# Sorting the second list of edges later, and idle products ahead of the first one, in a graph layer followed by a mixture of experts

## The chip, the cores and the metric

The kernel runs on 1 core of one Trainium2 chip. The metric is the device time of one launch in microseconds (us). Before the change it is 717.89 us, the median of three runs.

## The reference: what is computed

```python
x = x + gnn(layernorm(x), src, dst, edge_type)      # x: 625 x 512 float32; 10625 edges, 8 types
x = x + moe(layernorm(x))                           # 16 experts, top 2, 512 -> 1024 -> 512

def gnn(input, heads, tails, rel):
    h_self = input @ W_self.T + b_self
    H_all = einsum('rod,nd->rno', W_rel, input) + b_rel[:, None, :]     # 16 relations: 8 types x 2 ways
    agg = segment_sum(H_all[rel, tails], heads, 625) + segment_sum(H_all[rel + 8, heads], tails, 625)
    return relu(h_self + agg)

def moe(x):                                         # per expert e, combine = softmax over the top two
    out += combine[:, e] * ((silu(x @ gate[e]) * (x @ up[e])) @ down[e])
```

## The kernel before

A float32 matrix is split into a high part and a remainder, and three matmuls replace one float32 matmul. Two programs follow each other.

**The round** (0 to 388 us of the profile). The 625 nodes are five tiles of 125. There are 80 *products*, one for each of the 16 relations and 5 tiles: 12 matmuls of 512 columns into `p_h` (`product`, L837 to L858). ScalarE copies the result out (`take`, L689), writes the bias of the next but one product into the same bank (`bias_in`, L695), and rounds the weights of the next relation, a quarter per product (`w_main`, L680); VectorE subtracts for the remainder (`w_rest`, L507). SyncE stores the results in `h_dram` and loads weights.

Each edge belongs to two lists, one for each way. A list is sorted on the chip in these steps, `d` being 0 or 1:

- VectorE gives each edge its bucket (`buckets_of`, L433) and makes a one-hot tensor of it (`bucket_hots`, L442).
- TensorE sums that (`totals_of`, L827: 10 or 20 matmuls of one column) and ranks edges in their buckets (`ranks`, L813); VectorE reads the ranks (L490).
- VectorE computes places (`told_of`, `places`), then makes 85 pairs of one-hot columns (`column`, L535), which TensorE multiplies five at a time (`list_chunk`, L868). `read_list` (L546) turns the result into row numbers.

With the list, GpSimd gathers 190 blocks of 128 rows from `h_dram` (L409), up to 10 ahead; ScalarE and VectorE split them, and TensorE adds them up with a one-hot matrix (`message`, L879). Before product 0, VectorE also normalises the five tiles of x (`normal`, `scales`), TensorE transposes them (`turn_x`, L805), ScalarE takes the high part (`turned_high`, L672) and VectorE the low part (`low_columns`, L485).

**The order of all this is written out by hand.** Each engine has a loop over the 80 products, and tables say at which product a step is issued: `LISTS` (first product and columns per product), `START` and `PACE` (messages), `due` and `columns`. An engine executes in this order and waits at semaphores. Each product of relation j after its first one begins on VectorE with `w_rest`, which waits for ScalarE.

**The experts** (390 to 719 us) follow, with tokens sorted by expert and a loop over tiles of tokens.

A *block* of the program ends with a barrier of all engines; the round ends with a second one that clears its semaphores (L1038). The program has a loop around the round, which here runs once.

Of the kernel before, what the change touches and what calls it, by code (L numbers as in the profile page):

```python
# [40 lines left out]
LISTS = ((5, 5.5), (25, 3))  # L41

LAG, START, PACE = 4, 25, 3.0
# [24 lines left out]
def build(nc, x, edges, w_self, w_rel, biases, router_w, gate_w, up_w, down_w, out):  # L68
    ctx = ExitStack()
    with ctx:  # L70
# [108 lines left out]
        with ExitStack() as g:  # L179
# [63 lines left out]
            bucket_hot = rows_sb[0:EP, 0:3].rearrange("p a d -> p (a d)").bitcast(F16)[:, 0:BUCKETS * EC].rearrange("p (b c) -> p b c", b=BUCKETS)  # L243
            e_past = rows_sb[0:EP, 3, 0:len(SPANS) * EC].rearrange("p (n c) -> p n c", n=len(SPANS))
# [13 lines left out]
            p_totals = [p_list[0:EC, 0:2 * T], p_list[0:EC, 2 * T:BUCKETS]]  # L258
            p_counts = p_list[0:1, 128:128 + BUCKETS]
# [46 lines left out]
            def token_columns(a, t):  # L306

                return a[:, :, t * TP:(t + 1) * TP]

# [107 lines left out]
            def on_vector(dve, nth_round):  # L417
# [15 lines left out]
                def buckets_of(d):  # L433
                    in_way = [n for n, s in enumerate(SPANS) if s[0] == d]
                    for n in in_way[1:]:
                        i = v.tensor_scalar(e_past[:, n], e_type, float(SPANS[n][1]), None, ALU.is_ge)
                    then(i)
                    for n in in_way[1:]:
                        below = e_tile[:, d] if n == in_way[1] else bucket[:, d]
                        then(v.scalar_tensor_tensor(bucket[:, d], e_past[:, n], float(T), below, ALU.mult, ALU.add))  # L440

                def bucket_hots(d):  # L442
                    n_b = len(IN_WAY[d])
                    v.tensor_tensor(bucket_hot[:, IN_WAY[d].start:IN_WAY[d].stop], bucket[:, d].unsqueeze(1).to_broadcast([EP, n_b, EC]),
# [6 lines left out]
                def told_of(d):  # L451
# [7 lines left out]
                    for n in in_way[1:]:  # L459
                        c, c0 = SPANS[n][3], SPANS[n - 1][3]  # L460
                        i = v.scalar_tensor_tensor(first_block[:, d], e_past[:, n], float(T * c0), first_block[:, d], ALU.mult, ALU.add)
                        if c != c0:
                            i = v.scalar_tensor_tensor(held[:, d], e_past[:, n], float(P * (c - c0)), held[:, d], ALU.mult, ALU.add)
# [140 lines left out]
                dve.wait_ge(bias_hi, 1)  # L604
                v.tensor_tensor(bias_parts[LOW:LOW + BIASES], bias_f[LOW:LOW + BIASES], bias_parts[LOW:LOW + BIASES].bitcast(F32),
                                ALU.subtract).then_inc(bias_ready, 1)
                totals_of(1)
                dve.wait_ge(rest_loaded, 16)
                normal(2)
                scales(2)  # L610
                normal(3)
                scales(3)
                low_columns(2)
                ranks(0)
# [1188 lines left out]
```

## Time and profile before

| quantity | value |
|---|---|
| median of 3 runs | 717.89 us |
| lowest, highest run | 716.73, 722.73 us |
| the profiled execution: time, span | 720.36 us, 718.6 us |
| busy: TensorE, VectorE, ScalarE, GpSimd | 96%, 86%, 71%, 43% of the span |
| DMA over the span | 297 GB/s |
| mean granted clock of TensorE | 0.992 |

The span is that of one execution taken by the profiler; the time of the same execution is 1.8 us longer. Busy shares are averages over stages: TensorE is idle until 7.74 us and nearly always busy afterwards. A row of the timeline gives the start and the duration of one or several equal instructions; matmuls are pipelined, so the distance between two starts, not the duration, is what one costs.

### The profile page before, as it was taken

What the parts mean: (1) busy time and instruction counts of PE and PEld (TensorE: products, weight loads), DVE (VectorE), ACT (ScalarE), POOL (GpSimd) and SP (SyncE); (2) the same over time, 40 slices, a digit from 0 to 9 for tenths busy, and PEclk for the clock granted to TensorE, in tenths of its full rate; (3) what the DMA queues carried; (4) which work ended last, traced back from release to release, by engine and by line L of the source; (5) the groups of instructions that cost most, each with busy time, mean ns of one, the idle gap of its engine ahead of it and who ended that gap; (6) DMA issues with size and microseconds to landing.
All of it is one profiled execution on the core that took longest, in us unless ns stands there. A gap on an engine that the chain in (4) does not pass through costs nothing. (4 is left out here: it accounts for less than half of the span.)

```text
span 718.6 us, 10605 instructions
## 1 busy us (share of the span) xinstructions
PE 692.0 (96%) x3216; PEld 545.8 (76%) x3216; DVE 618.6 (86%) x1208; ACT 508.3 (71%) x722; POOL 306.5 (43%) x279
## 2 busy tenths in 40 slices
PE   5999999999999999999997989999999999999996
PEld 4777777777777777787755868788888888888884
DVE  8699979998999777777676889999999999999982
ACT  5646467766777777777556678888787888888881
POOL 3000048785877777777770033222221333333301
PEclk9999999999999999999998999999999999999998
DMA  8357579987988999988668979999999999999952
GB/s 252 107 171 264 166 220 318 307 279 243 303 280 284 326 307 305 304 282 247 202 202 289 358 232 390 407 406 401 405 369 405 378 375 383 363 390 368 355 200 30
DMA packets 60972, 213.33 MB, mean 297 GB/s; under 512 B 9485, under 2 KB 9882, under 8 KB 47870
## 3 DMA queue, kind: packets, MB, share of 16 engines
q1 hardware_dynamic: 41534, 154.43, 57.2%
q0 software_dynamic: 19392, 58.35, 27.7%
q8 instruction: 21, 0.34, 0.2%
q14 instruction: 25, 0.20, 0.1%
HBM read 184.46 MB, written 28.29 MB: 296 GB/s over the span
## 5 line engine op out<-in xcount | busy, mean ns | idle before, releaser
L409 POOL DMA_INDIRECT rows_sb<-h_dram,row_of x190 | 217.6, 1145 | 152.8 <-DVE row_of L554 89.4
L564 DVE TENSOR_TENSOR rows_lo<-rows_sb,rows_hi 128x512 fp32r<-128x512 f32 x175 | 120.0, 686 | 38.9 <-ACT rows_hi L706 38.4
L706 ACT CAST rows_hi<-rows_sb 128x512 fp32r<-128x512 f32 x175 | 106.3, 619 | 55.5 <-DMA rows_sb<-h_dram,row_of 51.3
L848 PE MATMUL p_h<-g_hi_sb,xt_hi_whole 128*125 128x512 f32 x320 | 129.0, 403 | 0.6 <-DVE xt_lo_whole L487 0.5
L849 PE MATMUL p_h<-g_lo_sb,xt_hi_whole 128*125 128x512 f32 x320 | 127.1, 397 | 0.0
L850 PE MATMUL p_h<-g_hi_sb,xt_lo_whole 128*125 128x512 f32 x320 | 127.0, 397 | 0.0
L1224 POOL DMA_INDIRECT tokens<-token_dram,rows_of_tokens x15 | 19.7, 1310 | 175.8 <-ACT rows_of_tokens L1530 135.4
L693 ACT COPY h_whole<-p_h 125x512 f32<-125x512 f32 x80 | 46.7, 583 | 51.6 <-PE p_h L850 46.6
L1278 DVE TENSOR_TENSOR u_lo_sb<-stage_up,u_hi_sb 128x2048 fp32r<-128x2048 f32 x34 | 76.4, 2285 | 0.9
L1278 DVE TENSOR_TENSOR d_lo_sb<-stage_down,d_hi_sb 128x2048 fp32r<-128x2048 f32 x32 | 71.9, 2286 | 3.8 <-ACT d_hi_sb L1515 3.8
L884 PE MATMUL p_sum<-rows_hi,seg_hot 128*125 128x512 f32 x175 | 71.4, 408 | 2.8 <-DVE rows_lo L564 2.5
L1652 PE MATMUL p_gate<-g_hi_sb,xt_lo_whole 128*128 128x512 f32 x256 | 74.1, 401 | 0.0
L1652 PE MATMUL p_up<-u_hi_sb,xt_lo_whole 128*128 128x512 f32 x256 | 72.7, 395 | 0.8 <-DVE u_lo_sb L1278 0.8
L1278 DVE TENSOR_TENSOR g_lo_sb<-stage_gate,g_hi_sb 128x2048 fp32r<-128x2048 f32 x32 | 71.8, 2283 | 0.7 <-ACT g_hi_sb L1515 0.7
L848 PEld LDWEIGHTS p_h<-g_hi_sb,xt_hi_whole 128*125 128x125 f32 x320 | 60.0, 188 | 15.7 <-ACT p_h L700 1.5
L850 PEld LDWEIGHTS p_h<-g_hi_sb,xt_lo_whole 128*125 128x125 f32 x320 | 59.9, 187 | 15.4
L849 PEld LDWEIGHTS p_h<-g_lo_sb,xt_hi_whole 128*125 128x125 f32 x320 | 60.0, 188 | 14.1
L1515 ACT CAST g_hi_sb<-stage_gate 128x2048 fp32r<-128x2048 f32 x32 | 60.1, 1912 | 14.7 <-DMA stage_gate<-in_L_ffn_gate_w 10.3
L540 DVE SCALAR_TENSOR_TENSOR told_whole<-block_iota,block_at,told 125x180 f16<-125x180 f16 (+1 forms) x170 | 69.2, 407 | 0.0
L885 PE MATMUL p_sum<-rows_lo,seg_hot 128*125 128x512 f32 x175 | 69.0, 394 | 0.0
L1515 ACT CAST u_hi_sb<-stage_up 128x2048 fp32r<-128x2048 f32 x34 | 63.7, 1913 | 2.1 <-DMA stage_up<-in_L_ffn_up_w 1.1
L1515 ACT CAST d_hi_sb<-stage_down 128x2048 fp32r<-128x2048 f32 x32 | 59.7, 1911 | 0.8 <-DMA stage_down<-in_L_ffn_down_w 0.8
(298 smaller groups left out, 1312.1 us busy)
## 6 DMA issues: line engine op xcount, KB each, us to landing
stage_up<-in_L_ffn_up_w SPq DMA_DIRECT2D x34, 1024.0 KB, 8.9
stage_gate<-in_L_ffn_gate_w SPq DMA_DIRECT2D x32, 1024.0 KB, 8.9
stage_down<-in_L_ffn_down_w SPq DMA_DIRECT2D x32, 1024.0 KB, 8.7
h_dram<-h_whole SPq DMA_DIRECT2D x80, 256.0 KB, 4.0
stage_up<-in_L_gnn_W_rel SPq DMA_DIRECT2D x64, 256.0 KB, 5.1
x_whole<-in_biases SPq DMA_DIRECT2D x16, 256.0 KB, 6.5
rows_sb<-h_dram,row_of POOLq DMA_INDIRECT x190, 5.2
stage_gate<-in_L_ffn_down_w SPq DMA_DIRECT2D x2, 1024.0 KB, 10.1
```

The lines of the kernel that those rows point to most:

```text
L409: q.indirect_dma_start(rows_sb[:, b % ROWS], None, h_dram[0:1 + made(n) * P], bass.IndirectOffsetOnAxis(ap=row_of[:, b:b + 1].bitcast(U32) ...
L540: i = v.scalar_tensor_tensor(told_hot[:, n % HOT_SETS, k, 0:2 * wide].rearrange("p (a b) -> p a b", a=2), block_iota[:, 0:wide].unsqueeze( ...
L564: v.tensor_tensor(rows_lo[:, b % PARTS], rows_sb[:, b % ROWS], rows_hi[:, b % PARTS].bitcast(F32), ALU.subtract).then_inc(part_lo, 1)
L706: s.copy(rows_hi[:, b % PARTS], rows_sb[:, b % ROWS]).then_inc(part_hi, 1)
L848: m.matmul(o, xt_hi[:, dc, at], wt_hi_sb[:, 1 - j % 2, dc], start=(by_matmul and dc == 0), stop=False, skip_group_check=True)
L849: m.matmul(o, xt_hi[:, dc, at], wt_lo_sb[:, 1 - j % 2, dc], start=False, stop=False, skip_group_check=True)
L850: last = m.matmul(o, xt_lo[:, dc, at], wt_hi_sb[:, 1 - j % 2, dc], start=False, stop=False, skip_group_check=True)
L884: m.matmul(o, seg_hot[:, b % HOTS], rows_hi[:, b % PARTS], start=False, stop=False, skip_group_check=True)
L885: m.matmul(o, seg_hot[:, b % HOTS], rows_lo[:, b % PARTS], start=False, stop=False, skip_group_check=True).then_inc(block_done, 1)
L1278: v.tensor_tensor(half(w_lo[k][:], k, i), staged(k, e, i), half(w_hi[k][:], k, i).bitcast(F32), ALU.subtract).then_inc(split_lo[k], 1)
L1515: s.copy(half(w_hi[k][:], k, i), staged(k, e, i)).then_inc(split_hi[k], 1)
L1652: i = m.matmul(into[:, h * 512:(h + 1) * 512], x_part[of_first(e)][:, c], w_part[k][:, c, h * 512:(h + 1) * 512], start=(c == 0 and x_part ...
```

## The change

- `totals_of(1)`, `buckets_of(1)` and `bucket_hots(1)` move from before product 0 to product 21 (`SECOND` is 20), `ranks(1)`, the counts and their reading from products 2 and 3 to products 22 and 23, `ranks(2)` from products 5 and 6 to 23 and 24, `told_of(1)` stays at 21, `places(1)` moves from 22 to 24. The number of rounds is computed at product 23.
- The one-hot tensor of the second list lies in `xn_whole`, which is free by then, and its sums in another bank. Hence `mark` and `carry_in`, which start the sums of messages in `p_sum`, move from products 8 to 12 to products 25 to 29.
- The first list's columns start at product 4 (5 before), messages at 24 (25 before).
- TensorE gets `keep_going`: float32 matmuls of 128 columns whose result is not used, 5 ahead of the round, 7 + 2 + 3 before product 0.
- What ran before the round is no longer a block of its own. The clearing barrier stands at the beginning of the round.
- The transposes of tiles 2, 3 and 4 stand in the middle of products 1, 2 and 3; ScalarE's and VectorE's early steps are in another order.

```diff
-LISTS = ((5, 5.5), (25, 3))
-
-LAG, START, PACE = 4, 25, 3.0
+LISTS = ((4, 5.5), (25, 3))
+
+LAG, START, PACE = 4, 24, 3.0
+SECOND, MARKS = 20, 25
...
+            def keep_going(n):
+
+                for _ in range(n):
+                    nc.tensor.matmul(p_h[:, 1, 0:P], ones[:], ones[:], start=True, stop=True)
...
                 scales(0)
                 scales(1)
-                buckets_of(1)
-                bucket_hots(1)
+                dve.wait_ge(bias_hi, 1)
+                v.tensor_tensor(bias_parts[LOW:LOW + BIASES], bias_f[LOW:LOW + BIASES], bias_parts[LOW:LOW + BIASES].bitcast(F32),
+                                ALU.subtract).then_inc(bias_ready, 1)
+                dve.wait_ge(rest_loaded, 16)
+                normal(2)
                 low_columns(0)
...
-                    if i == 3:
+                    if i == SECOND + 1:
+                        buckets_of(1)
+                        bucket_hots(1)
+                        dve.wait_ge(hot_ready, 2)
+                        told_of(1)
...
+                    if i == SECOND + 2:
+                        totals_of(1)
+                    if i == SECOND + 3:
+                        dve.wait_ge(counts_full, 1)
+                        then(v.tensor_copy(crow[:], p_counts))
                         ranks(1)
-                        dve.wait_ge(counts_full, 1)
-                        v.tensor_copy(crow[:], p_counts)
-                    if i == 6:
+                        round_count()
+                    if i == SECOND + 4:
                         ranks(2)
...
-                        if dc == KC - 2 and turned is not None:
+                        if dc == 1 and turned is not None:
                             turn_x(turned)
...
+                keep_going(7)
                 totals_of(0)
                 pe.wait_ge(totals_ready, 1)
                 ranks(0)
+                keep_going(2)
                 turn_x(0)
                 turn_x(1)
-                totals_of(1)
+                keep_going(3)
                 for i in range(PRODUCTS):
-                    if 8 <= i < 8 + T:
-                        mark(i - 8)
-                    product(i, i + 1 if i in (1, 2) else None)
-                    if i == 2:
+                    if MARKS <= i < MARKS + T:
+                        mark(i - MARKS)
+                    product(i, i + 1 if i in (1, 2, 3) else None)
+                    if i == SECOND + 1:
+                        pe.wait_ge(xt_ready, T)
+                        totals_of(1)
+                    if i == SECOND + 2:
                         pe.wait_ge(totals_ready, 2)
+                        m.matmul(p_counts, ones16[0:EC, 0:1], totals[:], start=True, stop=True).then_inc(counts_full, 1)
                         ranks(1)
-                        m.matmul(p_counts, ones16[0:EC, 0:1], totals[:], start=True, stop=True).then_inc(counts_full, 1)
-                        turn_x(4)
-                    if i == 5:
+                    if i == SECOND + 3:
                         ranks(2)
...
+            def before_rounds_on_tensor(pe):
+                pe.wait_ge(consts_ready, 2)
+                keep_going(5)
...
             with nc.Fori(0, rounds) as nth_round:
+                nc.all_engine_barrier(sems_to_clear=round_sems)
                 with nc.Block() as block:
...
-                nc.all_engine_barrier(sems_to_clear=round_sems)
```

Two places show how instructions move. The first is TensorE's beginning; a wait is named in brackets. Before:

```order
L1034 UNCONDITIONAL_BRANCH
L830 MATMUL p_list<-ones,rows_sb 85x1 [waits hot_ready]
L830 MATMUL p_list<-ones,rows_sb 85x1 x9
L819 MATMUL p_sum<-rows_sb,before 125x425 [waits totals_ready]
L820 MATMUL p_sum<-rows_sb,big 125x425
```

and now:

```order
L315 MATMUL p_h<-ones 128x128 [waits barrier_Pool_Activation_PE_DVE_SP_release,consts_ready]
L315 MATMUL p_h<-ones 128x128 x4
L1030 UNCONDITIONAL_BRANCH
L1050 UNCONDITIONAL_BRANCH [waits barrier_Pool_Activation_PE_DVE_SP_release]
L315 MATMUL p_h<-ones 128x128 x7
L838 MATMUL p_list<-ones,rows_sb 85x1 [waits hot_ready]
L838 MATMUL p_list<-ones,rows_sb 85x1 x9
L827 MATMUL p_sum<-rows_sb,before 125x425 [waits totals_ready]
```

Five idle matmuls stand ahead of the barrier and seven behind it, before the first step of the sort. The second place is product 21 on VectorE (`L513`, now `L520`, is `w_rest`). Before:

```order
L513 TENSOR_TENSOR g_lo_sb<-stage_up,g_hi_sb 128x512 [waits w_high]
L457 SCALAR_TENSOR_TENSOR bucket<-e_tile,edge 125x85 [waits edge_consts]
L461 SCALAR_TENSOR_TENSOR first_block<-rows_sb,first_block 125x85
L463 SCALAR_TENSOR_TENSOR held<-rows_sb,held 125x85
L461 SCALAR_TENSOR_TENSOR first_block<-rows_sb,first_block 125x85 [waits steps] x2
```

and now:

```order
L561 SCALAR_TENSOR_TENSOR row_of<-rel_of,p_list 128x90
L520 TENSOR_TENSOR g_lo_sb<-stage_up,g_hi_sb 128x512 [waits w_high,rows_ready]
L443 TENSOR_SCALAR xn_whole<-edge 125x85 x3
L447 SCALAR_TENSOR_TENSOR bucket<-xn_whole,e_tile 125x85 [waits steps]
L447 SCALAR_TENSOR_TENSOR bucket<-xn_whole,bucket 125x85 [waits steps] x2
L451 TENSOR_TENSOR xn_whole<-bucket,bucket_iota 125x1700 [waits steps]
L464 SCALAR_TENSOR_TENSOR bucket<-e_tile,edge 125x85 [waits edge_consts,hot_ready]
```

Seven instructions have come between `w_rest` and `told_of`. TensorE waits for the last of the seven behind the 12 matmuls of product 21:

```order
L858 MATMUL p_h<-g_hi_sb,xt_lo_whole 125x512
L838 MATMUL p_sum<-ones,xn_whole 85x1 [waits hot_ready,xt_ready]
L838 MATMUL p_sum<-ones,xn_whole 85x1 x19
L856 MATMUL p_h<-g_hi_sb,xt_hi_whole 125x512 [waits h_biased]
L857 MATMUL p_h<-g_lo_sb,xt_hi_whole 125x512
```

The 20 small matmuls and their wait stand between products 21 and 22.

## Rows read from the trace of the kernel before

**Rows 1.** The page: busy time, share of the span and instructions by engine.
```profile
PE 692.0 (96%) x3216; PEld 545.8 (76%) x3216; DVE 618.6 (86%) x1208; ACT 508.3 (71%) x722; POOL 306.5 (43%) x279
```

**Rows 2.** Timeline of TensorE's beginning: start, duration, engine, line, count, idle time before.
```profile
7.74 0.89 PE L830 MATMUL p_list<-ones,rows_sb 125*85 125x1 f16 x10 [7.74 <-DVE rows_sb L444]
...
13.72 1.63 PE L830 MATMUL p_list<-ones,rows_sb 125*85 125x1 f16 x20 [0.43 <-DVE rows_sb L444]
15.21 0.77 PE L848 MATMUL p_h<-g_hi_sb,xt_hi_whole 128*125 128x512 f32 x1
15.78 0.63 PE L849 MATMUL p_h<-g_lo_sb,xt_hi_whole 128*125 128x512 f32 x1
...
20.47 0.63 PE L835 MATMUL p_h<-bias_parts,select 128*125 128x512 f32 x1
...
21.26 0.39 PE L849 MATMUL p_h<-g_lo_sb,xt_hi_whole 128*125 128x512 f32 x1
21.49 0.40 PE L850 MATMUL p_h<-g_hi_sb,xt_lo_whole 128*125 128x512 f32 x1
```

**Rows 3.** Timeline of VectorE before product 0.
```profile
10.43 0.42 DVE L436 TENSOR_SCALAR rows_sb<-edge 125x85 f32<-125x85 int32 x3
...
13.58 0.67 DVE L487 TENSOR_TENSOR xt_lo_whole<-p_sum,xt_hi_whole 128x500 fp32r<-128x500 f32 x1
```

**Rows 4.** Timeline at the round's two ends, all engines.
```profile
4.64 1.28 ACT L734 ACT_TABLE_LOAD   x1 [0.39 <-PEq L971]
...
389.01 0.24 DVE L667 COPY logits<-p_list 125x80 f32<-125x80 f32 x1 [0.85 <-PE p_list L907]
...
390.58 0.78 PE L1721 MATMUL p_up<-xt_hi_whole 125*128 125x512 f32 x1 [2.47 <-PEq L1038]
```

**Rows 5.** Busy time by stretch: PE, PEld, DVE, ACT, POOL; granted clock; DMA share, GB/s.
```profile
12.00:16.00 4.00, 3.57 (x29) 3.08 (x28) 4.00 (x6) 3.51 (x7) 0.00 (x0) 1.00 0.99 311
...
390.00:392.00 2.00, 1.42 (x3) 1.01 (x4) 1.31 (x7) 1.43 (x2) 0.00 (x0) 0.50 0.43 139
...
396.00:398.00 2.00, 2.00 (x9) 1.56 (x7) 1.70 (x8) 0.64 (x2) 0.00 (x0) 0.84 0.98 217
```

**Rows 6.** Timelines of ScalarE and TensorE ahead of product 4.
```profile
31.48 0.57 ACT L674 CAST xt_hi_whole<-p_sum 128x500 fp32r<-128x500 f32 x1
31.94 1.14 ACT L687 CAST g_hi_sb<-stage_up 128x512 fp32r<-128x512 f32 x2
...
33.60 0.59 ACT L700 COPY p_h<-x_whole 125x512 f32<-125x512 f32 x1
...
34.24 0.49 PE L848 MATMUL p_h<-g_hi_sb,xt_hi_whole 128*125 128x512 f32 x1
```

**Rows 7.** Timelines of TensorE and VectorE at product 21.
```profile
90.84 0.48 PE L848 MATMUL p_h<-g_hi_sb,xt_hi_whole 128*125 128x512 f32 x1
...
92.09 0.69 DVE L513 TENSOR_TENSOR g_lo_sb<-stage_up,g_hi_sb 128x512 fp32r<-128x512 f32 x1 [1.69 <-ACT g_hi_sb L687]
92.70 0.24 DVE L457 SCALAR_TENSOR_TENSOR bucket<-e_tile,edge 125x85 f32<-125x85 f32 x1
```

**Rows 8.** Timeline: the first gather, and the wait of a message.
```profile
97.50 1.19 POOL L409 DMA_INDIRECT rows_sb<-h_dram,row_of  x1 [89.38 <-DVE row_of L554]
...
113.90 0.50 PE L884 MATMUL p_sum<-rows_hi,seg_hot 128*125 128x512 f32 x1 [0.51 <-DVE rows_lo L564]
```

**Rows 9.** Timeline of VectorE: first columns of list one, and its last.
```profile
37.85 0.23 DVE L539 TENSOR_SCALAR lane_whole<-slot_iota,lane 125x128 f16<-125x128 f16 x1
...
90.01 0.39 DVE L540 SCALAR_TENSOR_TENSOR told_whole<-block_iota,block_at,told 125x180 f16<-125x180 f16 x1
```

**Rows 10.** Waits, TensorE, 0 to 400 us: total, times, longest.
```profile
PE p_sum L884 <- DVE rows_lo L564: 2.5, 4, 0.9
PE p_sum L891 <- DMA rows_sb<-h_dram,row_of: 1.4, 1, 1.4
...
PE p_h L848 <- DVE xt_lo_whole L487: 0.5, 1, 0.5
```

More of the change, by code:

```diff
@@ L623, in on_vector @@
                     w_rest(1, dc)
+                dve.wait_ge(ranks_taken, 1)
+                places(0)
                 dve.wait_ge(edge_consts, 3)
@@ L636, in on_vector @@
                         then(v.tensor_tensor(place_in[:, 1], place_in[:, 1], rank_part[:], ALU.max))
-                    if i == 21:
-                        told_of(1)
-                        then(v.tensor_scalar(first[:], trip[:], 0.0, None, ALU.is_equal))
-                        v.tensor_tensor(select_self[:], select[:, 2 * R:2 * R + 1].bitcast(F32), first[:], ALU.mult).then_inc(self_ready, 1)
-                    if i == 22:
                         places(1)
@@ L736, in on_scalar @@
                 first_root(0)
+                act.wait_ge(bias_loaded, 16)
+                s.copy(bias_parts[:], bias_f[:]).then_inc(bias_hi, 1)
                 first_root(1)
@@ L828, in totals_of @@
                     pe.wait_ge(hot_ready, d + 1)
-                    for n, b in enumerate(IN_WAY[d]):
-                        i = m.matmul(p_totals[d][:, n:n + 1], bucket_hot[:, b], ones16[:, 0:1], start=True, stop=True)
+                    for n in range(len(IN_WAY[d])):
+                        i = m.matmul(p_totals[d][:, n:n + 1], bucket_hot[d][:, n], ones16[:, 0:1], start=True, stop=True)
                     i.then_inc(totals_full, 1)
@@ new lines, in before_rounds_on_sync @@
+            def before_rounds_on_sync(sp):
+                sp.sem_inc(up_loaded, 16)
+                sp.sem_inc(x2_stored, 16)
+                sp.dma_start(edge[:], edges).then_inc(edge_loaded, 16)
+                for some, loaded_some in ((slice(0, 2), x_loaded), (slice(2, T), rest_loaded)):
+                    sp.dma_start(x_all[:, some], x[:, some]).then_inc(loaded_some, 16)
+                sp.wait_ge(bias_cleared, 1)
+                sp.dma_start(bias_f[0:2 * LOW], biases).then_inc(bias_loaded, 16)
@@ new lines, in before_rounds_on_tensor, with before_rounds_on_scalar, before_rounds_on_vector @@
+            def before_rounds_on_tensor(pe):
+                pe.wait_ge(consts_ready, 2)
+                keep_going(5)
+            def before_rounds_on_scalar(act):
+                act.wait_ge(bias_cleared, 1)
+                for k in range(OUTS):
+                    nc.scalar.copy(h_whole[96:P, k], bias_f[96:P])
+            def before_rounds_on_vector(dve):
+                v = nc.vector
+                v.memset(carry[:], 0.0)
+                v.memset(trip[:], 0.0)
+            before_rounds_on_sync(nc.sync)
```

107 lines of the change are left out of this document (41 added, 66 removed).

## The prediction

> **What bounds the kernel now.** I read the page first, then the timeline of the round's start, then the waits. TensorE is busy for 96% of the span [rows 1], so a step that is taken off another engine gains nothing unless TensorE waited for it. From 15.21 us, where product 0 starts, to the last product TensorE hardly waits. What can be won lies in three places: before product 0, where TensorE stands until 7.74 us [rows 2]; in product 0 itself, whose matmuls follow each other at (20.47 - 15.78) / 11 = 0.43 us, while those from 21.26 us on follow at 0.23 us [rows 2]; and at the round's end, where 1.3 us lie between VectorE's last copy and TensorE's next matmul [rows 4]. Its other waits of the round are small: 2.5 us in all for split rows, mostly in the tail, and 1.4 us for one of the last gathers [rows 10]. The tail is paced by GpSimd's gathers, and those by the products before, so a shift of the products passes through to it. Both kernels issue the same messages from product 44 on.
>
> The 0.43 us per 512 columns are the lower of TensorE's two clock levels (1.2 GHz), 0.23 us the upper (2.4 GHz). The granted clock of the rows shows 1.00 at 12 to 16 us, where the matmuls themselves run at the lower level; behind the round's end it shows 0.50 [rows 5]. For the beginning I therefore go by distances between matmuls.
>
> **The change part by part.** Every term is TensorE's time, against the profiled execution of 720.36 us.
>
> *Start of product 0: -0.1.* Before, TensorE got to it at 15.21 us, behind the 20 one-column matmuls of the second list (13.72 to 15.21, with 0.43 us of waiting) [rows 2]. These go, and so do VectorE's 3.15 us of bucket work from 10.43 to 13.58 us [rows 3]. In their place VectorE gets the bias remainder and the statistics of tile 2, 1.7 us, which end before the transposed tile is there. Against this, a clearing barrier now stands ahead of the round. The block's own barrier costs about 0.4 us (ScalarE resumes at 4.64 us with 0.39 us of waiting); both together cost 390.58 - 389.25 = 1.33 us at the end [rows 4]. So the clearing one is worth about 0.9 us, and the start is 0.55 us later (it replaces the other). VectorE's chain then gives the first quarter of weights at 14.4 us; TensorE's own queue, if its idle products and transposes still run at the lower level, ends at 15.9 us. I take 15.1. Ends: -0.8 and +0.7.
>
> *Product 0 at the upper clock: -2.5.* Thirteen matmuls (12 and one for the bias) at 0.43 - 0.23, rounded. Ends: -2.5 and 0. The idle products are 17 float32 matmuls of 128 columns, a form the trace before does not show; I take 0.43 us each, the distance of the 512-column ones at the lower level, as an upper bound. They lie where TensorE was idle and cost nothing, unless the three last ones are late, which is in the term above.
>
> *The 20 small matmuls, now at product 21: +0.8.* 1.49 us before at the lower clock [rows 2]; half of it at the upper. Ends: +0.5 and +1.5.
>
> *Ranks, counts, marks: 0.* The same matmuls at the upper clock in both kernels, with TensorE saturated on both sides.
>
> *Product 4: +0.7 in all for products 1 to 4.* The transpose of tile 4 stood ahead of product 3 and is now in its middle. From there ScalarE has to do the high part (0.57), two quarters of weights (1.14), a copy out and the bias for product 4 (0.59 each): 2.9 us [rows 6], while TensorE has half a product left, 1.4 us. It waits 1.5 us. Before, that bias ended at 34.19 and product 4 started at 34.24, a wait of about 0.3 us [rows 6], and 0.5 us were lost before product 2 [rows 10]. Ends: 0 and +1.5.
>
> *Columns of list one: +0.3.* VectorE makes 85 in products 4 to 19 at 0.48 us, and 12 `w_rest` of 0.6: 48 us, against 50 us of TensorE. In the kernel before the 52.6 us from 37.85 to 90.4 [rows 9] contained the same, one more product and `ranks(2)`. VectorE begins later within its products, and is about level at product 19. Ends: 0 and +1.
>
> *Product 21: +3.1.* This is the largest cost. VectorE's steps of a product start with `w_rest`, and that waits for ScalarE, which first takes product 20 out. Before, product 21 starts at 90.84 and `w_rest` ends at 92.70 [rows 7], 1.86 us later. Without the double chunk between products 20 and 21, which leaves TensorE 0.73 us earlier relative to ScalarE, it is 2.6 us. Then come buckets and one-hots, 3.15 us [rows 3], ending 5.75 us after the product's start, plus 0.15 for the semaphore. The product is over after 12 x 0.23 = 2.8 us by the distance in [rows 2]. TensorE stands 3.1 us, with product 22 queued behind the wait. `read_list` and the first gathers are not delayed: they are issued at product 20. Ends: +2 and +4. Behind it, `told_of(1)` (2.5 us) and the copy of the totals end with product 22, so no second wait; the ranks are read within product 23. `mark(0)` waits for `ranks(2)` on VectorE, which ends just before.
>
> *Gathers and messages: -0.4.* The list is read before `told_of`, and a product earlier; the first gather was at 97.50 us and the messages then waited 0.51 and, in smaller pieces, 0.4 us [rows 8]. That goes. VectorE comes late with the first three messages, as `places(1)` stands ahead of them: +0.5. Ends: -1 and +0.5. Messages begin one product earlier, but their number by product 44 is the same.
>
> *Round's end: -0.9.* The clearing barrier leaves, the other stays [rows 4]. The experts' first steps all begin behind it. Ends: -1.3 and -0.3.
>
> Sum: -0.1 - 2.5 + 0.8 + 0.7 + 0.3 + 3.1 - 0.4 - 0.9 = +1.0 us, 721.4 for an execution like the profiled one. That one is 2.5 us above the median, so the median should be 717.9 + 1.0 = 718.9.
>
> **Two rules weighed.** Whether the clock is up at product 0 depends on what TensorE did before: in the kernel before it rose at 21 us, some 6 us into the products [rows 2]; behind the round's end it stood at 0.50 and came back within 396 to 398 us, whose mean is 0.84 [rows 5]. The Trainium skill, TensorE: Matmul & The Clock Gate, Part 1, says that the same kernel measures 6, 11 or 14 slow matmuls from run to run; by that the term of product 0 would not be 2.5 us but anything from 0 to 2.5, and the sum would be up to +3.5. No single trace here can show a spread. The second rule speaks against the change: the same page, section HAM oscillation, says that an idle wait between matmuls throttles the clock again, so that the next ones start slow. The trace agrees that it can happen: after 2.47 us of waiting [rows 4] the clock is 0.50 [rows 5].
>
> **The rivals.**
> - *The wait at product 21 isn't there* (faster). It is covered if VectorE finds the weights of product 21 ready. For it: the wait is made only of an order of two steps. Against it: [rows 7] show VectorE waiting 1.69 us for just these weights. It gives 718.9 - 3.1 = 715.8. 20%.
> - *The idle products don't bring the clock up in time*: the change doesn't do what it says. For it: a wait at the barrier, ten one-column matmuls and transposes lie among them, and in the kernel before a similar mixture from 7.74 to 15.21 us did not. It gives 718.9 + 2.5 = 721.4. 20%.
> - *The clock falls in product 21's wait* (slower than before). 3.1 us of standing plus 0.8 us of one-column matmuls resemble the 2.47 us ahead of the experts' first matmul. There it stayed low from 390.58 to about 396.6 [rows 4, 5], 6 us, of which half, 3 us, is lost. It gives 721.9, and decides if the wait is as long as at the round's end or longer. Against it: the wait of 1.44 us in the tail [rows 10] left the clock up. 15%.
>
> **Numbers.** The forecast case has 45%: 718.9, with its own range 717 to 721. The range for 8 in 10 takes in the first rival with its terms at their lower ends (714.5) and either slow rival with some more (723.5); both together, 724.4, are left out. About 1%, 7 us, is what a measurement of this kernel can tell from no change. No single case reaches it: faster by over 1% (below 710.7) 3%, slower (above 725.1) 4%, within 93%.
>
> **What would show it.** TensorE's first product starts near 15 us with matmuls 0.23 us apart. The 20 small matmuls at product 21 carry an idle time of about 3 us, put down to VectorE's one-hots; behind them matmuls are 0.23 us apart (0.43 if the clock fell). Product 5 starts near 33 us, product 44 within 2 us of where it was; the first gather is near 84 us; between VectorE's last copy and the experts' first matmul there is 0.5 us instead of 1.3. The prediction is wrong if product 44 moves by more than 4 us, or if the time changes in the experts.

## The result, and the profile after

| | before | changed |
|---|---|---|
| median of the first comparison, us | 717.5 (4 runs) | 730.01 (4 runs) |
| ratio, 95% interval | | 1.0152 [1.0115, 1.0188] |
| the same, two more comparisons | 717.75, 717.75 | 728.27, 726.24: 1.0149 [1.0116, 1.0182], 1.0115 [1.008, 1.0149] |
| first profiled execution: time, span, us | 720.36, 718.6 | 725.25, 723.5 |

The ratios come from all executions of a comparison, those over 1.5% above the fastest of their kernel left out (such as one of 770.83 us of e5 and one of 1390.03 us of e11 below), and are not quotients of the medians, which contain them all. By the ratios the change costs 8 to 11 us, by the medians 8.5 to 12.5. The forecast was 718.9, in a range of 714.5 to 723.5, with 4% on slower by over 1%: wrong.

The page of the changed kernel, busy time by engine:

```profile
PE 697.5 (96%) x3250; PEld 551.6 (76%) x3250; DVE 617.2 (85%) x1208; ACT 506.5 (70%) x722; POOL 307.2 (42%) x279
```

TensorE is busy 5.5 us more than in [rows 1]. The 34 new instructions are the 17 idle matmuls, two records each: up to 15 us TensorE is busy for 11.1 us, before for 6.6. That leaves 1.0 us for all the rest, in which what product 0 gains and what later stretches lose nearly cancel, so the page doesn't tell where the time went; the timeline does. The timeline of TensorE's beginning (start, duration, engine, line, count, idle time before):

```profile
14.38 0.47 PE L856 MATMUL p_h<-g_hi_sb,xt_hi_whole 128*125 128x512 f32 x1 [0.89 <-DVE g_lo_sb L520]
...
14.91 0.39 PE L858 MATMUL p_h<-g_hi_sb,xt_lo_whole 128*125 128x512 f32 x1
15.14 0.39 PE L856 MATMUL p_h<-g_hi_sb,xt_hi_whole 128*125 128x512 f32 x1
...
17.23 0.39 PE L843 MATMUL p_h<-bias_parts,select 128*125 128x512 f32 x1
...
29.32 0.49 PE L856 MATMUL p_h<-g_hi_sb,xt_hi_whole 128*125 128x512 f32 x1 [1.38 <-ACT p_h L707]
```

Product 0 runs at the upper clock and its bias matmul is at 17.23 us, 3.24 us before that of [rows 2]. Product 4 waits 1.38 us, as forecast. Then product 21, first TensorE, then VectorE:

```profile
87.26 0.40 PE L858 MATMUL p_h<-g_hi_sb,xt_lo_whole 128*125 128x512 f32 x1
90.77 1.55 PE L838 MATMUL p_sum<-ones,xn_whole 125*85 125x1 f16 x20 [3.11 <-DVE xn_whole L451]
92.18 0.77 PE L856 MATMUL p_h<-g_hi_sb,xt_hi_whole 128*125 128x512 f32 x1
92.75 0.63 PE L857 MATMUL p_h<-g_lo_sb,xt_hi_whole 128*125 128x512 f32 x1
```
```profile
86.78 0.69 DVE L520 TENSOR_TENSOR g_lo_sb<-stage_up,g_hi_sb 128x512 fp32r<-128x512 f32 x1 [3.50 <-ACT g_hi_sb L694]
87.39 0.42 DVE L443 TENSOR_SCALAR xn_whole<-edge 125x85 f32<-125x85 int32 x3
...
88.69 1.93 DVE L451 TENSOR_TENSOR xn_whole<-bucket,bucket_iota 125x1700 f16<-125x1700 f32 x1
```

The wait is the one forecast, 3.1 us. But from 92.75 us on matmuls are 0.43 us apart, and product 22 takes 5.39 us instead of 2.8. The 20 small matmuls are slow too: 1.41 us (90.77 to 92.18), where the forecast had 0.8. The busy time by stretch shows the clock (the number behind the last bracket), here and ahead of the first messages:

```profile
90.00:92.00 2.00, 1.23 (x18) 1.26 (x19) 1.86 (x8) 0.00 (x0) 1.70 (x2) 0.71 0.97 367
92.00:94.00 2.00, 2.00 (x9) 1.63 (x9) 1.90 (x9) 0.00 (x0) 1.70 (x2) 0.50 0.99 350
94.00:96.00 2.00, 2.00 (x6) 1.57 (x5) 0.17 (x2) 0.00 (x0) 1.39 (x3) 0.50 0.80 269
96.00:98.00 2.00, 2.00 (x7) 1.07 (x7) 0.00 (x0) 0.32 (x1) 1.47 (x2) 0.59 0.73 205
98.00:100.00 2.00, 2.00 (x23) 1.74 (x22) 0.53 (x1) 1.40 (x3) 0.00 (x0) 1.00 0.83 288
110.00:112.00 2.00, 0.94 (x3) 0.80 (x4) 2.00 (x7) 0.91 (x2) 1.60 (x2) 0.83 0.81 209
112.00:114.00 2.00, 2.00 (x7) 1.51 (x6) 2.00 (x7) 1.83 (x4) 1.50 (x1) 0.50 1.01 341
114.00:116.00 2.00, 2.00 (x9) 1.60 (x8) 2.00 (x7) 0.44 (x1) 1.89 (x1) 0.82 0.75 241
```

The second low stretch has its own wait, which the forecast did not see. TensorE and ScalarE behind product 25:

```profile
108.75 0.40 PE L858 MATMUL p_h<-g_hi_sb,xt_lo_whole 128*125 128x512 f32 x1
111.06 0.54 PE L892 MATMUL p_sum<-rows_hi,seg_hot 128*125 128x512 f32 x1 [1.91 <-ACT p_sum L733]
111.39 0.63 PE L893 MATMUL p_sum<-rows_lo,seg_hot 128*125 128x512 f32 x1
```
```profile
109.19 0.59 ACT L700 COPY h_whole<-p_h 125x512 f32<-125x512 f32 x1 [0.22 <-PE p_h L858]
109.81 0.59 ACT L707 COPY p_h<-x_whole 125x512 f32<-125x512 f32 x1
110.33 0.58 ACT L733 COPY p_sum<-carry 125x512 f32<-125x512 f32 x1
```

The first message needs the carry in its bank. `carry_in(0)` (L733) was issued at product 8 before, 17 products ahead of the first message; it now stands at product 25, behind `take(25)` (L700), which waits for TensorE's product 25, and behind `bias_in` (L707). TensorE finishes that product, and then waits until ScalarE has made two copies that the message doesn't need and the one that it does.

Of the messages, the group behind product 44 is the first that both kernels issue alike. It starts at 184.85 us before and at 192.53 after, 7.7 us late; the next group, behind product 45, at 189.50 and 197.18, as late. At the round's end:

```profile
394.79 0.24 DVE L674 COPY logits<-p_list 125x80 f32<-125x80 f32 x1 [0.29 <-PE p_list L915]
...
395.62 1.64 PE L1735 MATMUL p_up<-xt_hi_whole 125*128 125x512 f32 x3 [1.16 <-PEq L1032]
```

From the last copy to the experts' first matmul it is 0.83 us, where [rows 4] have 1.57. The experts begin 5.0 us later than before; the span is 4.9 us longer.

### The profile page after: what moved, and what is told of

Its sections match the earlier page's. It is cut to its first block and busy times, and to the rows that moved or that the text cites. A ratio compares the mean times of both kernels' runs of the same rounds, so it can differ in the third digit from the quotient of the medians.

```text
span 723.5 us, 10661 instructions
## 1 busy us (share of the span) xinstructions
PE 697.5 (96%) x3250; PEld 551.6 (76%) x3250; DVE 617.2 (85%) x1208; ACT 506.5 (70%) x722; POOL 307.2 (42%) x279
## 5 line engine op out<-in xcount | busy, mean ns | idle before, releaser
L416 POOL DMA_INDIRECT rows_sb<-h_dram,row_of x190 | 212.8, 1120 | 163.4 <-DMA h_dram<-h_whole 94.5
L713 ACT CAST rows_hi<-rows_sb 128x512 fp32r<-128x512 f32 x175 | 103.5, 617 | 26.9 <-DMA rows_sb<-h_dram,row_of 21.4
L700 ACT COPY h_whole<-p_h 125x512 f32<-125x512 f32 x80 | 46.9, 586 | 89.2 <-PE p_h L858 88.8
L1238 POOL DMA_INDIRECT tokens<-token_dram,rows_of_tokens x15 | 23.6, 1574 | 171.3 <-ACT rows_of_tokens L1544 132.3
```

The lines of the kernel that those rows point to most:

```text
L416: q.indirect_dma_start(rows_sb[:, b % ROWS], None, h_dram[0:1 + made(n) * P], bass.IndirectOffsetOnAxis(ap=row_of[:, b:b + 1].bitcast(U32) ...
L713: s.copy(rows_hi[:, b % PARTS], rows_sb[:, b % ROWS]).then_inc(part_hi, 1)
```

## Experiments

The changed kernel itself was run twice more, since its other times lay 2 to 9 us above that of its profiled execution. In the table, "45" is the start of the messages behind product 45 (those behind product 44 start 4.6 to 4.7 us earlier in every trace), "experts" that of the experts' first matmul, all in us, from the profiled execution. Kernels e1 to e4 were compared with a median before of 717.75, e7 to e9 with 718.48, e5, e10, e11 and e12 with 717.75 (another 29 runs). Two more runs, e13 and e14, were compared with medians of 745.95 and 748.95 and stand in the text.

| kernel | median | ratio to before, 95% | 45 | experts | span |
|---|---|---|---|---|---|
| before | 717.5 | | 189.50 | 390.58 | 718.6 |
| before, again (e6) | one run, 719.6 | | 188.43 | 389.05 | 717.7 |
| changed | 730.01 | 1.0152 [1.0115, 1.0188] | 197.18 | 395.62 | 723.5 |
| changed (e1) | 728.27 | 1.0149 [1.0116, 1.0182] | 198.74 | 394.66 | 724.3 |
| changed (e12) | 726.24 | 1.0115 [1.008, 1.0149] | 195.68 | 395.72 | 724.7 |
| 12 idle matmuls in the wait (e2) | 722.49 | 1.0044 [1.0018, 1.007] | 194.01 | 393.48 | 721.7 |
| 5 of them (e11) | 723.15 | 1.0076 [1.0045, 1.0107] | 194.10 | 395.80 | 724.9 |
| carry earlier (e3) | 724.49 | 1.0092 [1.0056, 1.0127] | 194.19 | 393.00 | 722.7 |
| one-hots earlier (e5) | 721.12 | 1.0045 [1.0012, 1.0078] | 189.21 | 388.62 | 718.5 |
| both earlier (e4) | 718.19 | 1.0002 [0.9976, 1.0028] | 189.28 | 385.70 | 714.3 |
| e4 without idle matmuls (e8) | 717.56 | 0.9978 [0.995, 1.0006] | 189.89 | 386.83 | 716.1 |
| e4, clearing barrier at the end (e9) | 718.32 | 0.9999 [0.9969, 1.0029] | 187.74 | 384.84 | 713.0 |
| e4, bias of product 4 earlier (e10) | 718.74 | 1.0007 [0.9982, 1.0033] | 189.19 | 388.49 | 717.4 |
| before + idle matmuls (e7) | 719.35 | 0.9998 [0.9967, 1.0028] | 189.53 | 393.76 | 722.7 |

**The changed kernel again (e1, e12).**

> The changed kernel once more, unchanged, to see what differs from run to run. Its first profiled execution was 725.3 us, three others 727.4 to 734.1. Theory (two waits of TensorE, each followed by a stretch at the lower clock): the waits of about 3.1 us at product 21 and 1.9 us ahead of the first message are there again and equally long, and only the lengths of the low stretches behind them differ; the time is 725 to 734. Rival (a slower tail or slower gathers in those runs): product 44's messages stand within 1 us of where they stood (about 8 us later than in the kernel before) and the difference arises behind them.

> The changed kernel a third time. Theory (the spread from run to run has two sources: the moment at which the clock first rises, 9 us or 13 us, which moves all products by 1.3 to 1.5 us, and the waits in the tail): the waits of 3.1 and 1.9 us and the two low stretches are there in this trace too, product 26 starts at 113.9 or at 115.4 us, give or take 0.2, and the median is 727 to 730 us. Rival (the low stretches differ in length from run to run): product 22 takes other than 5.3 to 5.5 us.

Both waits are in all three traces, 3.11 and 1.91 us to the hundredth. The low stretches are not: product 22 takes 5.39, 5.39 and 4.32 us, and behind the second wait the clock fell twice and stayed up once (e12's first messages take 1.47 us, those of the others 2.47 and 2.37). e12 by stretch:

```profile
92.00:94.00 2.00, 1.71 (x22) 1.65 (x23) 1.86 (x11) 0.00 (x0) 1.70 (x2) 0.72 0.99 355
94.00:96.00 2.00, 2.00 (x7) 1.50 (x6) 1.59 (x8) 0.00 (x0) 1.39 (x3) 0.50 0.93 308
96.00:98.00 2.00, 2.00 (x10) 1.38 (x9) 0.00 (x0) 0.27 (x1) 1.70 (x2) 0.93 0.77 205
```

So e1's theory holds, and e12's is refuted by its product 22 (4.32 us) and by the start of its product 26 (112.81 us, not 113.9 or 115.4); its median, 726.24 us, is below its range too. Besides the first rise of the clock (near 9 us in the first trace, near 13 us in the two others, 1.5 us for all products) the lengths of the low stretches differ from run to run.

**The wait at product 21, filled (e2, e11).**

```diff
                     if i == SECOND + 1:
                         pe.wait_ge(xt_ready, T)
+                        keep_going(12, p_sum[:, 2, 0:P])      # e11: 5
                         totals_of(1)
```

> The changed kernel with 12 idle matmuls of 128 columns in the wait at product 21, into a bank that nobody uses there; the wait of VectorE's one-hots stays. Theory (the fall of the clock costs by itself): TensorE still resumes the 20 small matmuls at the same time (within 0.3 us, near 90.8), but product 22 takes 2.8 us instead of 5.4, so product 23 and all behind it start 2.6 us earlier, and the time falls by 1.5 to 2.6 us. Rival (the standing alone costs, the clock would have fallen anyway or comes back at the same moment): product 22 still takes over 4.5 us and the time is within 0.7 us of the changed kernel.

> The changed kernel with 5 idle matmuls, not 12, ahead of the 20 one-column matmuls at product 21: about 1.2 us of the wait is filled and 1.9 us are left, as long as the wait ahead of the first message. Theory (a wait of this length does not lower the clock in a stretch that was busy before): product 22 takes 2.9 us as with 12, and the time is near 722.5 us. Rival (it does): product 22 takes over 4 us and the time is 725 us or more.

TensorE with 12, then with 5:

```profile
92.13 0.98 PE L838 MATMUL p_sum<-ones,xn_whole 125*85 125x1 f16 x20 [0.34 <-DVE xn_whole L451]
109.44 0.47 PE L892 MATMUL p_sum<-rows_hi,seg_hot 128*125 128x512 f32 x1 [1.91 <-ACT p_sum L733]
```
```profile
92.22 0.98 PE L838 MATMUL p_sum<-ones,xn_whole 125*85 125x1 f16 x20 [1.91 <-DVE xn_whole L451]
109.52 0.47 PE L892 MATMUL p_sum<-rows_hi,seg_hot 128*125 128x512 f32 x1 [1.91 <-ACT p_sum L733]
```

The 20 matmuls start within 0.2 us of e1 (92.34), in which the first products ran alike, so nothing was gained in waiting. The clock stays up: product 22 takes 2.96 us in both. It also stays up behind the second wait, whose length is unchanged. Hence the gain is larger than expected: 4.7 us at product 45 from e1 to e2, and 5.8 us between their medians, which come from the same comparison. That the standing alone costs is refuted. Five idle matmuls do as well in the trace (194.10 against 194.01); the ratios, 1.0076 and 1.0044, have intervals that overlap. In both traces, then, waits of 1.9 us left the clock up.

**The first message's carry (e3).**

```diff
+                    if MARKS <= i < MARKS + T:
+                        carry_in(i - MARKS)
                     take(i)
                     if i + 2 < PRODUCTS:
                         bias_in(i + 2)
-                    if MARKS <= i < MARKS + T:
-                        carry_in(i - MARKS)
```

> The changed kernel with ScalarE's copies of the carry (products 25 to 29) ahead of the copy-out of the product, not behind it. Theory (the first message waits for ScalarE, which first takes product 25 out): the wait of 1.9 us ahead of the first message goes, the clock does not fall there, and product 26 starts 3 to 3.5 us earlier relative to product 25; the time falls by 2 to 3.5 us. Rival (the first message would have to wait for something else, VectorE's split rows or the gather): a wait of 1 us or more stays in the same place under another name, and the time falls by less than 1 us.

```profile
90.65 1.60 PE L838 MATMUL p_sum<-ones,xn_whole 125*85 125x1 f16 x20 [3.11 <-DVE xn_whole L451]
109.49 0.47 PE L892 MATMUL p_sum<-rows_hi,seg_hot 128*125 128x512 f32 x1 [0.45 <-ACT p_sum L733]
```

Of 1.91 us 0.45 are left, the clock stays up behind it, and behind product 45 it is 3.0 us earlier than in the first trace of the changed kernel (product 20 within 0.2 us of it). Product 26 starts 5.2 us behind product 25 instead of 7.75, a gain of 2.5 us where 3 to 3.5 were expected; the median is 3.8 us below that of e1, from the same comparison, where 2 to 3.5 were. The cause is confirmed, and the rival (a wait of 1 us or more for something else) refuted.

**The wait at product 21, taken away (e5), and both (e4).** VectorE stands 3.5 us before `w_rest` of product 21 (the row of 86.78 us above), waiting for weights while TensorE is in products 20 and 21. There the buckets and one-hots find room:

```diff
                     if i == SECOND + 1:
-                        buckets_of(1)
-                        bucket_hots(1)
...
                             read_list(d)
+                            if d == 0:
+                                buckets_of(1)
+                                bucket_hots(1)
```

> The changed kernel with VectorE's buckets and one-hots of the second list at the end of product 20's steps; ScalarE's carry copies stay behind the copy-out. Theory (the wait at product 21 and the fall of the clock behind it cost 5.7 us; the wait ahead of the first message is 1.9 us and lowers the clock only where the clock had fallen shortly before): the wait at 21 is gone, the wait of 1.9 us ahead of the first message is there, matmuls behind it are 0.23 us apart, product 26 starts 7 us or more earlier than in the changed kernel, and the time is 719 to 722 us. Rival (each wait lowers the clock by itself): the messages behind the wait of 1.9 us take 2.4 us instead of 1.5, and the time is 1.5 us higher.

> The changed kernel with both waits taken away: VectorE's buckets and one-hots of the second list at the end of product 20's steps, in which it stands 3.5 us waiting for weights, and ScalarE's carry copies ahead of the copy-out. Theory (the two waits and the two falls of the clock are the whole difference): neither wait, nor low stretch between 84 and 120 us, product 44's messages within 1.5 us of the kernel before, 716 to 719 us in all, and runs that agree within 1%. Rival (there is a further loss, in the columns of list two, in the tail or in the gathers): over 720 us with the waits gone. Rival 2 (the one-hots at product 20 only move the wait, since weights for product 25 or columns come late): a wait of 1 us or more between products 20 and 26.

In e5 the wait at 21 is gone and the other stands alone:

```profile
104.63 0.47 PE L893 MATMUL p_sum<-rows_hi,seg_hot 128*125 128x512 f32 x1 [1.91 <-ACT p_sum L734]
```

The messages behind it take 1.48 us: the clock is up. Product 26 starts at 106.34, 7.6 us before the changed kernel's 113.95, and the median of 721.12 us is in the range of the theory. In e4 neither wait is left (0.45 us of the second) and no stretch from 84 to 120 us is below 1.00:

```profile
104.58 0.47 PE L893 MATMUL p_sum<-rows_hi,seg_hot 128*125 128x512 f32 x1 [0.45 <-ACT p_sum L734]
```

The median is 718.19 us, the ratio 1.0002 [0.9976, 1.0028]: within 2 us, the two waits and what the clock lost behind them are the difference between the kernels. The second rival is refuted too, as nothing new waits from 20 to 26.

**What the rest of the change is worth (e8, e9, e7, e10).** With both waits mended the kernel is still no faster than before, though the forecast had 2.5 and 0.9 us of gains in it.

> The version without the two waits (buckets at product 20, carry copies ahead of the copy-out), with its 17 idle matmuls taken out. Theory (they are worth the low stretch of product 0): product 0 runs at 0.43 us again, product 1 is 1.5 to 3 us later and the time rises by 1.5 to 3 us, to 720 to 721 us. Rival (a lead is given back in the tail): within 0.8 us of 718.2 us although product 1 is later.

e8 is e4 with its four `keep_going` calls removed. Product 0 is slow again only to 18.0 us:

```profile
17.59 0.57 PE L857 MATMUL p_h<-g_hi_sb,xt_hi_whole 128*125 128x512 f32 x1
18.00 0.40 PE L858 MATMUL p_h<-g_lo_sb,xt_hi_whole 128*125 128x512 f32 x1
```

The transposes in product 1 start at 20.80, in e4 at 20.13, in e3, e5 and e9, where the clock rose earlier, between 18.64 and 18.79. So in the traces the 17 matmuls bring 0.7 to 2.2 us there; in the time nothing is seen of it (ratio 0.9978 without, 1.0002 with), and the 1.5 to 3 us of the theory did not come. Whether the lead is given back in the tail, as the rival has it, is not shown: at product 45 e8 is 0.6 us behind e4, at the experts 1.1.

> The version without the two waits, with the clearing barrier back at the round's end and a plain one ahead of the round. Theory (the clearing barrier costs about 0.9 us wherever it stands, and at the end the experts pay it in full): the start of product 0 is 0.3 to 0.6 us earlier, the gap ahead of the experts' first matmul 0.7 to 1.3 us longer, the time 0 to 0.8 us longer. Rival (the shorter gap was eaten by something else in the experts): no change of the gap, or the time falls by 0.3 us or more.

```diff
+            nc.all_engine_barrier()
             with nc.Fori(0, rounds) as nth_round:
-                nc.all_engine_barrier(sems_to_clear=round_sems)
...
+                nc.all_engine_barrier(sems_to_clear=round_sems)
```

The round's first sums start at 7.94 us, 0.19 earlier than in e4 (8.13). The gap from VectorE's last copy to the experts is 1.57 us (383.27 to 384.84), in e4 0.82 (384.88 to 385.70). Product 0 starts at 14.16 us, in e3 and e5, with the same early clock, at 14.30, less than the 0.3 to 0.6 us expected. So the barrier's move gains 0.75 us at the end and pays 0.1 to 0.2 at the start; the clearing barrier doesn't cost the same wherever it stands. The time doesn't tell 0.5 us apart.

> The kernel before once more, unchanged: a second trace of it. Its profiled execution was 2.5 us above the median. Theory (the height of that execution lies in the tail, where TensorE waits for split rows and gathers): all products to the last stand within 1 us of where they stood, and what differs from execution to execution arises between 336 us and the experts' first matmul. Rival: product 1 or the clock ahead of it differs by over 1 us already.

The second trace of before refutes that all its spread is in the tail: its product 0 rises to the upper clock in the middle:

```profile
17.47 0.63 PE L850 MATMUL p_h<-g_hi_sb,xt_lo_whole 128*125 128x512 f32 x1
17.90 0.47 PE L848 MATMUL p_h<-g_hi_sb,xt_hi_whole 128*125 128x512 f32 x1
18.21 0.40 PE L849 MATMUL p_h<-g_lo_sb,xt_hi_whole 128*125 128x512 f32 x1
```

Product 1 starts at 19.61 us, in the trace that the forecast used at 20.90.

> The kernel before with the idle matmuls alone: 5 ahead of the round, 7 ahead of the first sums, 2 ahead of the transposes, 3 ahead of product 0; the second list's early steps stay where they were. Theory (the idle matmuls are worth the low stretch of product 0): matmuls of product 0 follow each other at 0.23 us, product 1 starts 2 to 3 us earlier (near 18.3), and the time falls by 1.5 to 2.8 us, to 715 to 716.3 us. Rival (a lead of the products is given back in the tail, which GpSimd's gathers pace): product 1 and product 44 are 2 us or more early, the waits between 336 and 370 us grow by as much, and the time is within 0.8 us of the kernel before.

e7 adds `keep_going` 5, 7, 2 and 3 to the kernel before, at the places of the change. Its TensorE:

```profile
13.84 0.98 PE L835 MATMUL p_list<-ones,rows_sb 125*85 125x1 f16 x20 [1.30 <-DVE rows_sb L449]
14.69 1.00 PE L313 MATMUL p_h<-ones 128*128 128x128 f32 x6
15.36 0.76 PE L853 MATMUL p_h<-g_hi_sb,xt_hi_whole 128*125 128x512 f32 x1
```
```profile
14.00:16.00 2.00, 2.00 (x28) 1.90 (x27) 2.00 (x4) 1.51 (x3) 0.00 (x0) 0.85 1.04 386
16.00:18.00 2.00, 2.00 (x6) 1.55 (x5) 1.97 (x4) 0.00 (x0) 0.00 (x0) 0.50 0.44 124
```

The clock had risen near 9 us and fell again behind a wait of 1.3 us for the second list's one-hots; product 0 is slow until 18.5. Neither theory nor rival was put to the test, so two more runs filled that wait (6 idle matmuls ahead of the second list's sums, 1 behind):

> The kernel before with the idle matmuls of the change, but 6 of them ahead of the second list's one-column matmuls and 1 behind, where 3 stood behind: the wait of 1.3 us in which the clock fell in the kernel with idle matmuls alone (product 0 at 0.43 us until 18.6 us) is filled. The second list's early steps stay where they were, so there is neither a wait at product 21 nor a new one ahead of the first message. Theory (the idle matmuls gain what product 0 loses at the lower level, 1.3 to 2.6 us, if no wait stands between them and product 0): product 0 runs at 0.23 us, product 1 starts near 18.3 us, products and messages up to the last are 1 to 2.5 us ahead of the kernel before, and the time is 715.5 to 717 us. Rival (such a lead is lost in the tail or within the spread of it): product 1 is early, but the time is within 0.8 us of the kernel before.

> The kernel before with 6 idle matmuls in the wait of 1.3 us, unchanged from the run before it, on another chip: on the first one both kernels were 28 us slower than on the chips used till then, nearly all of it from 200 us on, where messages waited for split rows. Theory (product 0 at the upper clock is a gain that reaches the end): 715.5 to 717 us against some 717.8 of the kernel before, ratio 0.998 or less. Rival (lost in the tail): ratio 0.999 to 1.001, although product 1 starts 1 us or more earlier.

```profile
15.94 0.48 PE L853 MATMUL p_h<-g_hi_sb,xt_hi_whole 128*125 128x512 f32 x1
16.26 0.40 PE L854 MATMUL p_h<-g_lo_sb,xt_hi_whole 128*125 128x512 f32 x1
```

These rows are e13's. Its product 0 runs at the upper clock, its bias matmul is at 18.82 us (20.47 and 19.38 in the traces of before), and product 1 starts at 19.05, in e14 at 18.32 (20.90 and 19.61 before): the wait, filled, left the clock up in both. The messages behind product 45 are at 188.98 in e13, within 0.6 us of both traces of before. The medians are 747.17 and 749.19 us, but in these comparisons the kernel before took 746 and 749 us too (e13 waited 21.1 us for split rows from 200 us on, and e14's messages behind product 45 start at 196.18 only): ratios 0.9996 [0.9953, 1.0039] and 1.0016 [0.9957, 1.0075]. No gain is seen, but one of 2 us isn't excluded.

> The version without the two waits, with ScalarE's copy-out of product 2 and bias of product 4 ahead of the transposed tile 4 and of all four quarters of the next weights: takes away TensorE's wait of 1.4 us at product 4. Theory (that wait is lost time of TensorE): product 5 starts 1.2 to 1.5 us earlier and so does all behind it; 716.5 to 717.3 us. Rival (VectorE is saturated from product 4 to 19 and sets when the first list ends): product 5 is earlier, but TensorE's wait for one-hot columns at product 19 grows from 0.5 to 1.5 us or more, and the time is within 0.5 us of 718.2 us.

```diff
                 scaled(4)
-                for dc in range(2):
-                    w_main(1, dc)
+                take(2)
+                bias_in(4)
                 turned_high(4)
-                for dc in range(2, KC):
+                for dc in range(KC):
                     w_main(1, dc)
-                for i in range(2, PRODUCTS):
+                for i in range(3, PRODUCTS):
```

The rival holds but for a size: the waits for columns grow to 1.4 us in two waits, where it had 1.5 in one. Waits of TensorE up to 120 us, first of e4, then of e10:

```profile
PE p_h L857 <- ACT p_h L708: 1.4, 1, 1.4
...
PE p_list L884 <- DVE told_whole L547: 0.5, 1, 0.5
```
```profile
PE p_list L884 <- DVE told_whole L547: 1.4, 2, 0.9
...
PE p_h L857 <- DVE xt_lo_whole L494: 0.2, 1, 0.2
```

Product 4 starts at 29.43 instead of 30.60 us. But the wait comes back for one-hot columns: product 20 starts at 83.04 us, in e4 at 83.12. VectorE is busy for 39.2 of the 40 us from 40 to 80 us in e4 and 39.3 in e10, in the kernel before for 37.0.

## Why the forecast was wrong

The prediction gave a sign of its own for being wrong, product 44 moving by more than 4 us; it moved by 7.7. Two terms that it put at nothing did it, the fall of the clock behind product 21's wait and the carry copy on ScalarE.

- **Start of product 0, -0.1:** 14.38 against 15.21, 0.8 us early in the first trace; 15.92 in e1 and 15.91 in e12, 0.7 us late. Both lie at the ends of the bounds, and the moment of the clock's first rise decides which. The clearing barrier, put at 0.55 us here, cost 0.1 to 0.2 (e9).
- **Product 0, -2.5:** right for the trace it was read from (20.90 - 15.21 = 5.69 us before, 17.46 - 14.38 = 3.08 after), too high as an average, and taken from the one trace where the low stretch was longest. Against the second trace of before, product 0 of the changed kernel gains 1.3 us (4.41 to 3.08). The rule weighed there, that the number of slow matmuls differs from run to run (the Trainium skill, TensorE: Matmul & The Clock Gate, Part 1), agrees with the traces: slow until 21.3, 18.2 and 18.0 us in before, e6 and e8.
- **The 20 small matmuls, +0.8:** 0.85 us at the upper clock (92.13 to 92.98 in e2), as forecast. In the changed kernel the clock was already falling: 1.41, 1.32 and 1.01 us.
- **Product 4, +0.7:** the wait of 1.4 us is there. e10 showed that it costs nothing in the end, as VectorE sets the end of the first list. The step that failed here is the one that added this wait to TensorE's time. It belongs to the term "columns of list one" (+0.3), which had VectorE "about level": VectorE is the bound there.
- **Product 21's wait, +3.1:** 3.11 us measured, cause and size.
- **The clock behind it:** this is the first step that failed. The sum put it at nothing ("the 20 small matmuls" at the upper clock, product 22 at 0.23 us per matmul); it stood as a rival at 15%, with 3 us. It came in all four traces with the wait (product 22 took 2.6, 2.6, 1.5 and 2.5 us more), and e2, in which the wait is filled, shows that the fall costs by itself. The argument against it was a wait of 1.44 us in the tail that left the clock up, which says nothing of 3.1. The nearer row was the one ahead of the experts, 2.47 us and a fall [rows 4, 5], which was named and outvoted. The rule that an idle wait lowers the clock (the Trainium skill, TensorE: Matmul & The Clock Gate, HAM oscillation) agrees with all four: 3.11 us, then 0.50. Even this rival, 721.9 us, lies below all three medians.
- **Ranks, counts, marks, 0, and gathers and messages, -0.4:** the second step that failed, and not among the rivals. The change moved `carry_in` to product 25; the forecast put "marks" at nothing on TensorE and didn't ask what stands ahead of the copy on ScalarE. It cost 1.9 us of waiting and, in two traces of three, some 1.4 us of low clock. The first gather was at 84.49 us, near 84 as forecast.
- **Round's end, -0.9:** the gap shrank by 0.75 us, inside the bounds.

The forecast without the barrier's gain gives +1.9 us at products 44 and 45. With 2.6 for the first fall, and 1.9 and 1.4 for the second wait and its fall, that is 7.8; the first trace shows 7.7. So what was left out accounts for the lag, though the closeness is partly luck: product 0 started 0.7 us earlier than the term had it, and the small matmuls took 0.6 us more. Over three traces of the changed kernel and two of before, the lag at product 45 is 197.2 - 189.0 = 8.2 us; the times differ by 8 to 11. The rest is located in part only. From the messages behind product 45 to the end of the span the traces of the table take 525.0 to 533.2 us. TensorE's waits for split rows and gathers from 200 us on are 0.5 us in e1, 2.0 in the first trace of the changed kernel and 4.4 in e7. And the clock is low around the experts' start for 7 to 10 us in most traces, but for some 17 in e7 (533.2) and 14 in e11 (530.8), where it fell behind a wait of 2.95 and of 2.13 us for one of the last gathers; e7's:

```profile
383.84 1.86 PE L896 MATMUL p_sum<-rows_sb,lane_whole 128*125 128x512 f32 x2 [2.95 <-DMA rows_sb<-h_dram,row_of]
```

That spread also hides the 1 to 2 us that e4, e7 and e9 should show.

## What to carry to other kernels

When a step is moved next to its user, look at what stands ahead of its last copy on every queue that it passes: a copy behind the copy-out of the current product makes the matmul engine wait for itself. A wait of 3 us on TensorE should be priced at about one and a half times its length or more, since the clock fell behind it each time (3.1 us cost 1.5 to 2.6 more here), and where the work can't be had earlier, a few idle matmuls save that addition (five did in e11). And take the low stretch of a start from several traces: one trace showed 2.5 us where another had 1.3.

## What the runs showed of the hardware

- Waits of 3.1 us on a TensorE that was busy before lowered the granted clock to 0.50 in 4 of 4 traces; waits of 1.9 us at product 21 or ahead of the first message in 0 of 4 (e2, e5, twice e11). The same 1.9 us lowered it in 2 of 3 traces of the changed kernel, where a low stretch had ended some 12 us earlier. But an earlier fall isn't needed either. e14's TensorE stood for 2.11 us (for something that the row doesn't name) behind some 100 us at the upper clock, and it fell, as it did behind 1.98 us at 226.95 us in e13, while waits of 1.92 us at 235.14 in the first trace of the changed kernel and 1.94 us at 227.23 in e5 left it up. e14's TensorE, and its stretch behind the wait:

```profile
123.42 0.49 PE L889 MATMUL p_sum<-rows_hi,seg_hot 128*125 128x512 f32 x1 [2.11 <-issue]
```
```profile
124.00:126.00 2.00, 2.00 (x6) 1.60 (x5) 2.00 (x8) 0.20 (x1) 1.70 (x2) 0.50 0.82 259
```

- A wait of 1.3 us was enough in e7, behind transposes and some 4 us after the clock had first risen. So a wait near 2 us can go either way, and the length alone doesn't decide; what does was not isolated. The theories of e5 and e11, that 1.9 us lower the clock only behind an earlier fall, hold for their own traces, not as a rule.
- With nearly the same instructions the clock first rose near 8 or 9 us in six traces with idle matmuls and near 13 us in seven. Between traces of one kernel that shifts product 0 by 1.0 to 1.5 us (14.97 in e14 and 15.94 in e13; 14.38, 15.92 and 15.91 in the three of the changed kernel).
- In the comparisons of e13 and e14 the kernel before took 746 and 749 us, 4% more than in all others. The second ran on the chip on which e6 to e9 had been compared, with 718.5 us then. In e13's trace, from 200 to 378 us, ScalarE's copy-out of the product (`take`) waits for neither TensorE nor another engine in six waits of 24.4 us in all, up to 6.5 us each (in e14's in five, 20.7 us in all), which the two traces of the kernel before, from other comparisons, don't have; ScalarE's share of splitting the rows stands behind it in its order. Besides the product, this copy waits only for the store of an earlier result to `h_dram`. That these stores landed late is argued from the code, and why is open.
